# Two graph layers and a Mamba block: convolution in place, z moved behind the time step, C rows one at a time, a fifth ring slot

## The reference

```python
def layer0(h, adj):                       # degree-normalised graph convolution
    d = adj.sum(1) ** -0.5
    return relu(((adj * d[:, None] * d[None, :]) @ h) @ W.T + b)

def layer1(h, adj):                       # graph convolution, layer norm, Mamba
    h = relu(adj @ h @ gcn_w + gcn_b)
    h = layernorm(h) * ln_g + ln_b
    xc, z = split(h @ w_in)               # 256 channels each
    u = silu(causal_conv4(xc) + conv_b)   # 4 taps along the 8192 rows
    dt_in, B, C = split(u @ w_xp)         # 8, 16, 16 columns
    dt = softplus(dt_in @ w_dt + b_dt)
    dA, dBu = exp(dt * A), dt * B * u     # 8192 x 256 x 16
    # scan over the rows: state = dA * state + dBu;  y = sum over 16 states of state * C
    y = (y + u * D_skip) * silu(z)
    return y @ w_out

x = x + layer0(relu(layernorm(x)), adj)
x = x + layer1(relu(layernorm(x)), adj)
```

## Time and profile before

| | us |
|---|---|
| median of 3 runs (2560.52 to 2565.92) | 2564.95 |
| the profiled execution | 2565.95 |
| its span | 2564.1 |
| TensorE busy | 2202.8 |
| VectorE busy | 1998.2 |
| GpSimd busy | 1027.8 |
| ScalarE busy | 970.2 |

### The profile page before, as it was taken

How to read it: one execution, slowest core, us unless ns; L and a number is a source line. 1 busy time by engine, 2 the same in 40 slices (tenths; PEclk the granted TensorE clock), 3 DMA queues, 4 the chain that set the end, 5 groups by cost and what they waited for, 6 DMA issues and landing times.

```text
span 2564.1 us, 21768 instructions
## 1 busy us (share of the span) xinstructions
PE 2202.8 (86%) x6736; PEld 1242.6 (48%) x6736; DVE 1998.2 (78%) x2000; ACT 970.2 (38%) x1696; POOL 1027.8 (40%) x549
## 2 busy tenths in 40 slices
PE   0336788999999999999999988898889888889776
PEld 0112334444447888888886444444444444444333
DVE  7899998897545666565654489888988988889996
ACT  0000000000014555555553455555555555555552
POOL 1101110111000000000000288888889888889665
PEclk9968899999999999999999999999999999999998
DMA  9999999999756656565555688888898788887221
GB/s 392 411 419 421 421 419 388 389 395 360 258 232 242 219 209 223 189 223 189 206 190 171 223 269 279 261 258 262 266 270 267 250 271 261 253 270 231 79 75 49
DMA packets 133090, 683.36 MB, mean 267 GB/s; under 512 B 14928, under 2 KB 15728, under 8 KB 80880
## 3 DMA queue, kind: packets, MB, share of 16 engines
q1 hardware_dynamic: 110592, 604.02, 63.0%
q0 software_dynamic: 5616, 40.90, 7.7%
q10 hardware_dynamic: 16768, 37.05, 4.0%
HBM read 624.76 MB, written 16.25 MB: 250 GB/s over the span
## 4 chain that ended last, share of the span: by engine, by line
PE 40%; POOL 30%; issue 12%; DMA 10%; DVE 6%; ACT 2%; POOLq 0%; ACTq 0%; SPq 0%; DVEq 0%
PE ps L929 21%; PE ps L848 14%; POOL arena L544 10%; POOL ring L544 10%; DMA ring<-adj 6%; DVE arena L668 5%; DMA arena<-adj 4%; POOL arena L550 2%; PE ps L969 2%; POOL arena L537 1%; POOL arena L559 1%; POOL arena L532 1%; POOL ring L550 1%; POOL ring L559 1%; ACT diag_h L1087 1%
## 5 line engine op out<-in xcount | busy, mean ns | idle before, releaser
L969 PE MATMUL ps<-ring,diag_h 128*128 128x512 f32 x1152 | 559.3, 620 | 66.2 <-DMA ring<-adj 64.1
L929 PE MATMUL ps<-adj_parts,h_parts 128*128 128x512 f32 x2592 | 595.0, 391 | 4.1 <-ACT adj_parts L1144 3.7
L929 PEld LDWEIGHTS ps<-adj_parts,h_parts 128*128 128x128 f32 x2592 | 485.7, 188 | 110.8 <-ACT adj_parts L1144 6.2
L668 DVE TENSOR_TENSOR arena<-arena,ring 128x2048 f32<-128x2048 f32 x180 | 412.3, 2291 | 60.0 <-DMA ring<-adj 48.7
L848 PE MATMUL ps<-ring,arena 128*128 128x512 f32 x824 | 382.7, 623 | 54.8 <-DMA ring<-adj 54.8
L969 PEld LDWEIGHTS ps<-ring,diag_h 128*128 128x128 f32 x1152 | 224.1, 199 | 324.9 <-issue 239.4
L765 DVE TENSOR_TENSOR ps<-arena,ps 128x1024 f32<-128x1024 f32 x256 | 310.1, 1211 | 86.3 <-POOL arena L532 56.8
L687 DVE TENSOR_TENSOR adj_parts<-ring,adj_parts 128x1024 fp32r<-128x1024 f32 x216 | 264.1, 1225 | 97.3 <-ACT adj_parts L1144 86.6
L1220 ACT ACTIVATE arena<-arena,a_sb 128x512 f32<-128x512 f32 x512 | 338.4, 708 | 0.5
L544 POOL TENSOR_TENSOR arena<-arena 128x1024 f32<-128x1024 f32 x130 | 313.6, 2470 | 61.5 <-ACT state L1212 61.4
L499 POOL TENSOR_SCALAR nmr<-mv 128x8 f32<-128x8 f32 (+1 forms) x32 | 23.9, 746 | 766.3 <-DVE mv L593 765.0
(11 more groups left out here) (107 smaller groups left out, 2128.0 us busy)
## 6 DMA issues: line engine op xcount, KB each, us to landing
ring<-adj SPq DMA_DIRECT2D x452, 1024.0 KB, 11.1
arena<-c_scratch SPq DMA_DIRECT2D x128, 512.0 KB, 4.7
diag_h<-adj SPq DMA_DIRECT2D x32, 1024.0 KB, 12.7
arena<-adj SPq DMA_DIRECT2D x28, 1024.0 KB, 16.3
arena<-arena POOLq DMA_DIRECT2D x13, 1024.0 KB, 13.1
arena<-ring POOLq DMA_DIRECT2D x13, 1024.0 KB, 13.1
ring<-ring POOLq DMA_DIRECT2D x13, 1024.0 KB, 13.1
arena<-x ACTq DMA_DIRECT2D x16, 512.0 KB, 7.6
```

Source lines behind the costliest of these rows:

```text
L668: nc.vector.tensor_tensor(acc, acc, v, ALU.add).then_inc(adds_done, 1)
L929: last = nc.tensor.matmul(acc[:, c, :], h_parts[:, blk % 2, layer, h_part, a * F:(a + 1) * F], adj_parts[:, buf, adj_part, c * MM:(c + 1) ...
L969: last = nc.tensor.matmul(acc_c[k % 2] if k >= 2 else y_ps[:, k, :], tile_of(h1, PJ * p + j), blk[:, j * T:(j + 1) * T], start=first and j ...
```

## The change

1. The convolution goes from PSUM straight into u, which has three buffers; its SiLU, the skip connection and the gate work in place on u. `cv` and `yg` are gone.
2. SiLU is split: SILU_U at -10, SILU_Z at -3. The z products move to -5 and -4; for chunk 0 to slots 0 and 1, and its SiLU to slot 3.
3. DBC, SPLIT, DT and SOFTPLUS come two slots earlier, WEIGHTED_U one slot, to -4. NORMALISE comes three slots later, GATE one.
4. C rows are loaded one by one, one in each slot, into four buffers of one row, where there were three of two.
5. The half adds stand at n = 7, 11, 14 (HALF_ADD), after the issue of the next accumulating DMA in the same slot; `quad_in` is two semaphores in turn.
6. The ring has five slots in this stage; one pair of state buffers moves to the space set free.
7. The planner gives slots -6 to -1 one matmul pair each, and spreads the rest from slot 0 on.

```diff
-RING_C = 4
+RING_C = 5
-GCN, BIAS, STATS, AGGREGATE, NORMALISE = -26, -25, -23, -19, -18
-TRANSPOSE, XZ, SILU, DBC, SPLIT = -14, (-13, -11, -9, -8), -8, -7, -6
-DT, SOFTPLUS, WEIGHTED_U = -5, -4, -3
+GCN, BIAS, STATS, AGGREGATE, NORMALISE = -26, -25, -23, -19, -15
+TRANSPOSE, XZ, SILU_U, SILU_Z, DBC, SPLIT = -14, (-13, -11, -5, -4), -10, -3, -9, -8
+DT, SOFTPLUS, WEIGHTED_U = -7, -6, -4
 QSUM, NSUM = (11, 11, 10, 8), 6
-LOAD_X1, SKIP, GATE, OUT, RESIDUAL, STORE = 22, 21, 22, 30, 32, 33
+HALF_ADD = (7, 11, 14)
+LOAD_X1, SKIP, GATE, OUT, RESIDUAL, STORE = 22, 21, 23, 30, 32, 33
+SILU_Z0 = 3
-CSB = 3
+CSB = 4
...
+def xz_at(g, c):
+    if c >= HALVES and g == c - HALVES:
+        return 0
+    k = chunk_at(g, XZ[c])
+    return None if k == 0 and c >= HALVES else k
...
-        if g > DBC:
+        if g >= 0:
             room = sum(max(SLOT_US - small_us(h), 0) for h in range(g, end))
             due += (len(rest) - n - due) * max(SLOT_US - small_us(g), 0) / room
         else:
-            due += n < len(units[1])
+            due += n < len(units[1]) or g > DT
...
-        cv = work2(HALVES, T)
-        u = [work2(HALVES, T) for _ in range(2)]
+        u = [work2(HALVES, T) for _ in range(3)]
-        csb = [work2(2, T) for _ in range(CSB)]
-        yg = work2(HALVES, T)
+        csb = [work2(T) for _ in range(CSB)]
...
-                pair = (g + 4) // 2
-                if g % 2 == 0 and 0 <= pair < NCH * DS // 2:
-                    k, n = divmod(2 * pair, DS)
-                    if pair == 0:
-                        sp.wait_ge(s1_ready, 2)
+                row = g + 3
+                if 0 <= row < NCH * DS:
+                    k, n = divmod(row, DS)
                     sp.wait_ge(c_out, 16 * (k + 1))
-                    if pair >= CSB:
-                        sp.wait_ge(mult_done, 2 * (pair - CSB) + 2)
-                        sp.wait_ge(c_in[pair % CSB], 16 * (pair // CSB))
-                    sp.dma_start(csb[pair % CSB], c_dram[k:k + 1, n * T:(n + 2) * T]...
+                    if row >= CSB:
+                        sp.wait_ge(mult_done, row - CSB + 1)
+                        sp.wait_ge(c_in[row % CSB], 16 * (row // CSB))
+                    sp.dma_start(csb[row % CSB], c_dram[k:k + 1, n * T:(n + 1) * T].to_broadcast([P, T]))\
+                        .then_inc(c_in[row % CSB], 16)
...
-                    if k < QUAD_CHUNKS and n % 4 == 2 and n >= 6:
-                        q = g // 4 - 1
-                        pool.wait_ge(quad_in, 16 * (q - k + 1))
-                        first, second = (hs[(4 * q + j) % HSB] for j in range(2))
-                        nc.gpsimd.tensor_tensor(first, first, second, ALU.add).then_inc(quad_done, 1)
                     if k < QUAD_CHUNKS and n % 4 == 3 and n < DS - 4:
                         pool.wait_ge(mult_done, g + 1)
                         pool.dma_start(hs_pairs[(g // 2 - 1) % (HSB // 2)], hs_pairs[g // 2 % (HSB // 2)],
-                                       accum_op=ALU.add).then_inc(quad_in, 16)
+                                       accum_op=ALU.add).then_inc(quad_in[(g // 4 - k) % 2], 16)
+                    if k < QUAD_CHUNKS and n in HALF_ADD:
+                        q = QUADS * k + HALF_ADD.index(n)
+                        pool.wait_ge(quad_in[(q - k) % 2], 16 * ((q - k) // 2 + 1))
+                        first, second = (hs[(4 * q + j) % HSB] for j in range(2))
+                        nc.gpsimd.tensor_tensor(first, first, second, ALU.add).then_inc(quad_done, 1)
...
                     if h == 0:
                         dve.wait_ge(nsum_done, sums(k, DS - 1))
-                        if k:
-                            dve.wait_ge(misc_full, misc_at["out", k - 1] + 1)
-                    nc.vector.scalar_tensor_tensor(yg[:, h, :], u[k % 2][:, h, :], cols_sb[:, 2, h:h + 1],
+                    nc.vector.scalar_tensor_tensor(u[k % 3][:, h, :], u[k % 3][:, h, :], cols_sb[:, 2, h:h + 1],
                                                    y_ps[:, h, :], ALU.mult, ALU.add).then_inc(y_free, 1)
...
-                nc.scalar.activation(u[k % 2], cv, ACT.Silu).then_inc(u_ready, 1)
+                nc.scalar.activation(u[k % 3], u[k % 3], ACT.Silu).then_inc(u_ready, 1)
...
+                        if c == 0 and k >= 3:
+                            act.wait_ge(misc_full, misc_at["out", k - 3] + 1)
-                        evacuate((f"xz{c}", k), cv[:, c, :], bias=cols_sb[:, 0, c:c + 1], scale=1.0)
+                        evacuate((f"xz{c}", k), u[k % 3][:, c, :], bias=cols_sb[:, 0, c:c + 1], scale=1.0)
...
-                k = chunk_at(g, SILU)
-                if k is not None:
-                    if k:
-                        silu_u(k)
+                k = chunk_at(g, SILU_U)
+                if k:
+                    silu_u(k)
+                k = 0 if g == SILU_Z0 else chunk_at(g, SILU_Z) or None
+                if k is not None:
                     evacuated(act, "xz3", k)
                     nc.scalar.activation(sz[k % 2], sz[k % 2], ACT.Silu).then_inc(sz_ready, 1)
```

More of the change, by code:

```diff
@@ L200, in build @@
     for g in range(FIRST_SLOT, LAST_SLOT):
-        for stage, kinds in ((GCN, ["gcn"]), (OUT, ["out"]), (TRANSPOSE, ["tr"]), (XZ[0], ["xz0"]), (XZ[1], ["xz1"]),
-                             (XZ[2], ["xz2"]), (XZ[3], ["xz3"]), (DBC, ["dbc"]), (DT, ["dt0"]),
+        for stage, kinds in ((GCN, ["gcn"]), (OUT, ["out"]), (TRANSPOSE, ["tr"]), (DBC, ["dbc"]), (DT, ["dt0"]),
                              (DT + 1, ["dt1"])):
@@ L206, in build @@
                 misc += [(kind, k) for kind in kinds]
+        misc += [(f"xz{c}", xz_at(g, c)) for c in range(2 * HALVES) if xz_at(g, c) is not None]
     misc_at = {key: m for m, key in enumerate(misc)}
@@ L371, in build @@
         pair_done = sem("pair_done")
-        quad_in = sem("quad_in")
+        quad_in = [sem(f"quad_in{i}") for i in range(2)]
         quad_done = sem("quad_done")
@@ L463, in _ @@
             for g in slots:
-                pair = (g + 4) // 2
-                if g % 2 == 0 and 0 <= pair < NCH * DS // 2:
-                    k, n = divmod(2 * pair, DS)
-                    if pair == 0:
-                        sp.wait_ge(s1_ready, 2)
-                    sp.wait_ge(c_out, 16 * (k + 1))
-                    if pair >= CSB:
-                        sp.wait_ge(mult_done, 2 * (pair - CSB) + 2)
-                        sp.wait_ge(c_in[pair % CSB], 16 * (pair // CSB))
-                    sp.dma_start(csb[pair % CSB], c_dram[k:k + 1, n * T:(n + 2) * T].rearrange("a (n t) -> a n t", n=2)
-                                 .to_broadcast([P, 2, T])).then_inc(c_in[pair % CSB], 16)
+                row = g + 3
+                if 0 <= row < NCH * DS:
+                    k, n = divmod(row, DS)
+                    sp.wait_ge(c_out, 16 * (k + 1))
+                    if row >= CSB:
[3 more added lines that the diff above has]
+                        .then_inc(c_in[row % CSB], 16)
                 while q < len(loads) and block_end.get(last_in_slot[q], g) <= g:
@@ L531, in _ @@
                     pool.wait_ge(u_ready, k + 1)
-                    nc.gpsimd.tensor_tensor(w[k % 2], dt[k % 2], u[k % 2], ALU.mult).then_inc(w_ready, 1)
+                    nc.gpsimd.tensor_tensor(w[k % 2], dt[k % 2], u[k % 3], ALU.mult).then_inc(w_ready, 1)
                 k = chunk_at(g, GATE)
@@ L536, in _ @@
                     pool.wait_ge(sz_ready, k + 1)
-                    nc.gpsimd.tensor_tensor(yg, yg, sz[k % 2], ALU.mult).then_inc(yg_ready, 1)
+                    nc.gpsimd.tensor_tensor(u[k % 3], u[k % 3], sz[k % 2], ALU.mult).then_inc(yg_ready, 1)
                 if 0 <= g < NCH * DS:
@@ L541, in _ @@
                     pool.wait_ge(state_saved, g + 1)
-                    pool.wait_ge(c_in[g // 2 % CSB], 16 * (g // (2 * CSB) + 1))
-                    c_row = csb[g // 2 % CSB][:, g % 2:g % 2 + 1, :].to_broadcast([P, HALVES, T])
+                    pool.wait_ge(c_in[g % CSB], 16 * (g // CSB + 1))
+                    c_row = csb[g % CSB].unsqueeze(1).to_broadcast([P, HALVES, T])
                     nc.gpsimd.tensor_tensor(buf, buf, c_row, ALU.mult).then_inc(mult_done, 1)
                     k, n = divmod(g, DS)
-                    if k < QUAD_CHUNKS and n % 4 == 2 and n >= 6:
-                        q = g // 4 - 1
-                        pool.wait_ge(quad_in, 16 * (q - k + 1))
-                        first, second = (hs[(4 * q + j) % HSB] for j in range(2))
-                        nc.gpsimd.tensor_tensor(first, first, second, ALU.add).then_inc(quad_done, 1)
                     if k < QUAD_CHUNKS and n % 4 == 3 and n < DS - 4:
@@ L1027, in _ @@
                         for h in range(HALVES):
-                            last = nc.tensor.matmul(m_ps[:, t * F:(t + 1) * F], yg[:, h, t * P:(t + 1) * P],
+                            last = nc.tensor.matmul(m_ps[:, t * F:(t + 1) * F], u[k % 3][:, h, t * P:(t + 1) * P],
```

(4 more changed lines are left out.)

## The result

| | before | after |
|---|---|---|
| median of the runs, us | 2562.73 (4 runs) | 2472.83 (4 runs, 2469.93 to 2477.7) |
| ratio after / before | | 0.965 (0.9629 to 0.967) |
| span of the profiled execution, us | 2564.1 | 2471.0 |

The change gives 3.5%, some 90 us.

What follows compares the result with a forecast made beforehand. The prediction took GpSimd, with its wait for the accumulating DMA, to set the pace. Its terms, -56.8 - 12 - 11.4 + 17 = -63.2 us, led from 2565.95 to 2502.7, as a median 2502 us, range 2474 to 2545.

Steps and rivals of the forecast that it cites:

- GpSimd and its DMA as the cause: Scan: GpSimd's work plus its 7.65 us a chunk waiting for the accumulating DMA sets the 69.47 us pace.
- Half adds, "of 7.65 us some 1 is left": Scan, GpSimd: moving half adds behind the DMA issue leaves some 1 of 7.65 us of waiting a chunk.
- w, -56.8 us: Scan, VectorE: w one slot earlier removes its waits for w, -56.8 us over the whole scan.
- The waits for B rows, "I take half, -12 us": Scan, VectorE: fifth ring slot against SyncE's added waiting; between 0 and -24.2 us, half taken, -12 us.
- C rows one by one, "+17 us": Scan, GpSimd: single rows landing late cost 1.3 us a chunk, +17 us in 13 chunks.
- rival 1: Scan: GpSimd bound behind C rows landing in 9 us, chunk 68.0 us, 2536 us in all; chance 0.20.
- Start, -11.4 us: Start of the scan: shorter chain and fewer queued matmul pairs, first product at 1437.6 instead of 1449.01, -11.4 us.
- Products put off, 0: Scan, TensorE: 16 postponed matmul pairs add 1.05 us a chunk, staying below VectorE's 62.9: 0; uncovered +13.9 us.
- the ceiling by VectorE of 62.9 us: Scan: VectorE would need 62.9 us a chunk without its waits for w and B rows.
- two ways to one floor: Scan, VectorE: 62.9 us a chunk without waits, and chunk 14's 62.84 us, taken as agreeing on one floor.
- z behind the time step, 0: Scan, ScalarE: two more table loads a chunk, covered by dA made two slots ahead: 0; uncovered 14 us.
- rival 4: Whole kernel: everything goes, waits for w and B rows and the start's 11.4 us, giving 2474 us; chance 0.10.

Runs made afterwards that it cites:

- e4: The kernel before with only the half adds moved to n = 7, 11, 14 behind the DMA issue, with two semaphores: 2477.42 us, ratio 0.9654.
- e1: The changed kernel with the half adds back at n = 6, 10, 14, ahead of the next DMA issue: 2586.54 us, ratio 1.0077 to the kernel before.
- e3: The changed kernel with w (WEIGHTED_U) back at -3 instead of -4: 2480.65 us, ratio 0.9667 to the kernel before.
- e2: The changed kernel with a ring of four slots instead of five (RING_C = 4): 2475.68 us, ratio 0.9646 to the kernel before.
- e7: The changed kernel with six single C row buffers instead of four and a ring of four slots: 2474.66 us, ratio 0.9651 to the kernel before.
- e5: The changed kernel with three C row buffers instead of four, a row asked for one slot later: 2543.36 us, ratio 0.9926 to the kernel before.
- e10: The changed kernel with SPARED = 1 instead of 3, so chunks 13 and 14 are also summed by quads: 2469.41 us, ratio 0.9632 to the kernel before.
- e12: The changed kernel itself, measured again with nothing altered: 2473.21 us, ratio 0.9645 to the kernel before.

## Why the prediction was wrong

The step that failed is an overlap. The prediction took VectorE's period without its waits, 62.9 us, and added to it in full a wait of GpSimd, the C rows' +17 us, though GpSimd needs only 61.8. And it gave back only half of the waits for B rows, an effect of the cause that it had found itself. The terms one by one:

*GpSimd and its DMA as the cause: right.* e4 and e1 show it from both sides.

*Half adds, "of 7.65 us some 1 is left": right in the main;* 1.1 / 12 = 0.1 us a chunk are left.

*w, -56.8 us: the size was right, its attribution not.* The 54.4 us were a symptom. They go with the half adds alone (e4), and w's earlier place is worth 7 us at most (e3).

*The waits for B rows, "I take half, -12 us": mis-sized by 7 us.* In the stretch, 24.2 us became 5.0, so -19. The prediction had itself said that TensorE's waits for blocks came from GpSimd's lag, and then split the effect as if the ring slot and the new wait in SyncE might settle it. e1 has both, and waits 69.3 us for B rows; e2 has no fifth slot and waits 8.1 in all.

*C rows one by one, "+17 us": mis-sized by all of its 17 us, the larger error.* That a row lands late was right. Issue and landing in the stretch, count, KB, median us:

```profile
arena<-c_scratch SPq DMA_DIRECT2D x192, 256.0 KB, 8.1
```

That is above the 7.0 us that the prediction's count allowed. By that count the ten rows of a chunk in which GpSimd catches up would take (8.1 + 2.8) / 4 = 2.73 us each instead of 2.33, so 4 us of waiting a chunk; there were 11.3 / 12 = 0.9. The count left out the other work between the multiplies. After w at 1873.29 the same timeline has

```profile
1875.61 2.62 POOL L550 TENSOR_TENSOR arena<-arena 128x1024 f32<-128x1024 f32 x1
...
1880.20 2.34 POOL L550 TENSOR_TENSOR arena<-arena 128x1024 f32<-128x1024 f32 x1
...
1884.95 2.36 POOL L550 TENSOR_TENSOR arena<-arena 128x1024 f32<-128x1024 f32 x1
...
1889.58 2.35 POOL L550 TENSOR_TENSOR arena<-arena 128x1024 f32<-128x1024 f32 x1
...
1896.75 9.30 POOL L550 TENSOR_TENSOR arena<-arena 128x1024 f32<-128x1024 f32 x4
...
1907.04 4.96 POOL L550 TENSOR_TENSOR ring<-ring,arena 128x1024 f32<-128x1024 f32 x2
1912.66 2.36 POOL L550 TENSOR_TENSOR ring<-ring,arena 128x1024 f32<-128x1024 f32 x1 [0.67 <-DMA arena<-c_scratch]
```

At first multiplies start 4.6 to 4.8 us apart, and a row has 14 us. Then come four and two bare ones, and only behind them a wait of 0.67 us. That this spacing is all of the reason is read from the timeline, not tested.

The waits that were left cost no time, and here lies the overlap. GpSimd's chunk without DMA waits was 61.8 us, as rival 1 says, VectorE's 62.9. So a wait of 1.1 us a chunk on GpSimd is free; with the prediction's own 1.3 GpSimd would need 63.1, which is +3 us in 13 chunks and not +17. The runs showed 0.9 a chunk, and e7, which has none, is no faster. With three rows (e5) the waits are well above that room, and 70 us of time; there the same count had put 150. The Trainium skill's ring order (DMA: Bandwidth & Descriptors, "Queues, rings and completion order"), cited beside this term, is in keeping with rows that land in 8.1 us with 256 KB, but no run here tells the order from the load on the DMA engines; it decided nothing.

*Start, -11.4 us: measured -7.8.* u was ready at 1428.15 and not at 1427.3, by what came ahead of the chain. From the table load of the first SiLU to the first product it is 24.06 us before and 15.40 after, so -8.7. In the chain four matmuls (L1059, now L1063) took 3.35 us instead of 1.93, and the ten records of adjacency products 0.62 each instead of 0.44, both at the granted clock of 0.76. So w ended at 1439.22 and not at 1437.6, and the first B row came late by another 1.69 us. The term took its durations from a stretch at the upper clock. In the 14 us TensorE was busy 10.48, where it had been busy 18.44 of 20; but that the thinner plan brought the clock down is not shown. e4, with the start and the products of the kernel before, had a clock of 0.75 from 1430 to 1444 us, busy 13.22 of 14, and took 28.24 us where that kernel took 24.06. e3 and e7, with the thin plan, had 0.88, four matmuls in 1.96 us, and 13.8 us in all. What moves the clock between them is open.

*Products put off, 0, and the ceiling by VectorE of 62.9 us: right.* Chunks take 63.04. But of the "two ways to one floor" only the first is one. The second was chunk 14, with 62.84 us; there VectorE had less to do, 57.98 us instead of 61.7, and that the two agree is chance. The busy table of the kernel before:

```profile
2413.00:2476.00 63.00, 47.92 (x123) 22.02 (x122) 57.98 (x51) 35.94 (x66) 42.01 (x20) 0.95 0.23 76
```

TensorE's slower clock had been read as an upper end, and the upper clock did come back: 979 records of 592 ns where 944 took 624.

*z behind the time step, 0: right.* ScalarE is busy 38 us more over twelve chunks (493.97 for 455.85). GpSimd waits 1.8 + 0.6 us for its copy of the state, where before it was too late to wait at all; the matmuls and VectorE wait less for ScalarE than before. The table loads in the stretch are 24 + 12 + 12 = 48 before (L1220, L1205, L1294), and now

```profile
L1224 ACT ACT_TABLE_LOAD x36 | 46.2, 1283 | 0.6
L1278 ACT ACT_TABLE_LOAD x13 | 16.7, 1283 | 0.2
L1209 ACT ACT_TABLE_LOAD x12 | 15.4, 1283 | 0.2
L1301 ACT ACT_TABLE_LOAD x12 | 15.4, 1283 | 0.2
```

*What had no term.* With the terms as measured, -56.8 for w, -18.9 for B rows (29.1 - 7.2 over the scan, less 3.0 at the start), -7.8 for the start and 0 for C rows, the sum is -83.5 us, and the spans differ by 93.1. Of the other 9.6 the largest parts are on VectorE: its waits ahead of the split (L831, now L835) for ScalarE's copy fell from 10.6 to 4.4 us, 0.6 of it at the start, and its busy time by 3.7 us in all. Which part of the change did it isn't shown. So rival 4 met the time in part by luck: its start and B rows were some 9 us too large, and these 9.6 made up for it.

As to the chances: with the cause found and VectorE's floor computed, the sum took 2.5 us a chunk back on two unmeasured costs, and the floor itself got only 0.10. Open is what makes the four chunks from w of chunk 5 to w of chunk 9 longer than most (63.9 to 65.1 us; 63.4 to 65.5 in e10 and e12); it wasn't tried.

## What to carry to other kernels

When an engine's busy time and one kind of wait add up to the whole period, that wait is the price, here nearly one to one, until the next engine's floor. Waits that others have for that engine are effects and must not be costed as parts of their own. Cost each engine's period by itself and take the longest: a wait on an engine that is not the longest is free up to the difference, here 1.1 us a chunk, and must not be added to another engine's floor. Moving a waiting instruction behind work that is due anyway was worth more here than buffers, prefetch and reordering together, and taking 2.4 us out of a transfer's shadow cost some 22 to 26 us. A buffer ring is costed by all that the consumer does between two uses, not by the one instruction that uses it; where the count comes near, one buffer can decide, as four and three rows did here.
